# First attention of a graph network: TensorE's step in another order, key sums a step ahead of their scores, value sums five tiles behind

## The reference

```python
enh = x + 0.1 * query_emb
Q, K, V = (enh @ Wq + bq), (enh @ Wk + bk), (enh @ Wv + bv)      # 4 heads of 64
mod_k = K[src] + 0.2 * rel_w[edge_type][:, None, :]
scores = einsum('ehd,ehd->eh', Q[dst], mod_k) / 8
w = softmax of scores over the edges of one dst
agg = segment_sum(w[:, :, None] * V[src], dst)
x = layernorm(x + layernorm(agg @ Wo + bo + x) * gamma + beta)
```

## Time and profile before

| what | value |
|---|---|
| median of 3 runs | 4586.03 us (4585.14 to 4588.12) |
| profiled execution | 4583.4 us, of which span 4581.9 us |
| tiles of the first attention | 521, POOL's first gather at 350.35 us, its last at 2407.72 us |
| PE, DVE, ACT, POOL busy over the whole span | 81%, 74%, 61%, 68% |

### The profile page before, as it was taken

The page is one execution under the profiler, slowest core; times in us unless marked ns, Lnnn a source line. Parts: engine busy times, 40 slices in busy tenths (PEclk is TensorE's granted clock), DMA queues, the critical chain, the costliest instruction groups (busy, mean ns, idle before and its releaser), DMA issues. The chain is left out here.

```text
span 4581.9 us, 149697 instructions
## 1 busy us (share of the span) xinstructions
PE 3730.9 (81%) x42462; PEld 2550.6 (56%) x42462; DVE 3401.2 (74%) x11603; ACT 2779.6 (61%) x7985; POOL 3137.5 (68%) x3229
## 2 busy tenths in 40 slices
PE   6987988888888888888886877877777888778774
PEld 4654555555555555555554655555555555556553
DVE  3225788777887778877775677788877888877787
ACT  2324555555555555555553777777777777777775
POOL 1227777777777777777772777777777777777773
PEclk9998999999999999999997678777777777876876
DMA  6878998999999999898983777777777777777774
GB/s 204 281 246 238 267 267 263 264 264 264 265 263 265 263 265 266 262 265 263 265 266 100 193 206 210 204 204 206 204 207 208 204 206 206 204 207 209 204 207 129
DMA packets 820557, 1052.06 MB, mean 230 GB/s; under 512 B 458633, under 2 KB 632338, under 8 KB 820464
## 3 DMA queue, kind: packets, MB, share of 16 engines
q0 software_dynamic: 225072, 726.83, 54.0%
q1 hardware_dynamic: 594078, 323.35, 27.4%
q10 hardware_dynamic: 1314, 0.99, 0.1%
HBM read 915.79 MB, written 133.39 MB: 229 GB/s over the span
## 5 line engine op out<-in xcount | busy, mean ns | idle before, releaser
L1286 POOL DMA_INDIRECT plain_rows<-xp,plain_index x1563 | 1559.9, 998 | 555.3 <-issue 438.8
L765 POOL DMA_INDIRECT typed_rows<-kv,typed_index x1563 | 1505.2, 963 | 586.1 <-issue 444.4
L1391 PE MATMUL plain_p_o<-plain_rows,plain_weight_t 128*64 128x130 f32 (+1 forms) x8336 | 855.1, 348 | 43.3 <-DVE plain_weight_t L1417 42.5
L1158 ACT ACTIVATE typed_weight<-typed_weight,typed_col 128x416 f32<-128x416 f32 x521 | 334.7, 642 | 860.5 <-DVE typed_col L990 811.4
L1378 PE MATMUL plain_p_s<-all_cst,plain_rows 128*128 128x128 f32 (+1 forms) x2084 | 453.2, 316 | 360.0 <-DMA plain_rows<-xp,plain_index 358.1
L1391 PEld LDWEIGHTS plain_p_o<-plain_rows,plain_weight_t 128*64 128x64 f32 (+1 forms) x8336 | 569.5, 168 | 202.2 <-issue 128.7
L874 PE MATMUL typed_p_s<-typed_kt,typed_q 64*32 64x416 f32 x4168 | 471.6, 519 | 251.8 <-issue 223.4
L1378 PEld LDWEIGHTS plain_p_s<-all_cst,plain_rows 128*128 128x128 f32 (+1 forms) x2084 | 334.4, 173 | 513.2 <-issue 495.6
L988 DVE CUSTOM_DVE_ANT_0 typed_weight<-typed_p_s,typed_far 128x416 f32<-128x416 f32 x521 | 305.5, 586 | 339.5 <-PE typed_p_s L874 313.4
L1424 DVE CUSTOM_DVE_ANT_0 plain_alpha<-plain_alpha,plain_far 128x416 f32<-128x416 f32 x521 | 309.8, 595 | 309.6 <-ACT plain_alpha L1540 296.9
L961 DVE TENSOR_TENSOR typed_kt<-typed_p_kt,typed_rel 128x768 f32<-128x768 f32 x521 | 494.2, 949 | 4.0 <-PE typed_p_kt L851 3.8
(11 more groups left out here) (191 smaller groups left out, 6299.7 us busy)
## 6 DMA issues: line engine op xcount, KB each, us to landing
typed_match<-match SPq DMA_DIRECT2D x131, 208.0 KB
plain_match<-match SPq DMA_DIRECT2D x131, 208.0 KB
agg<-qkv_zero SPq DMA_DIRECT2D x98, 264.0 KB
typed_agg<-agg SPq DMA_DIRECT2D x98, 264.0 KB
plain_agg<-agg SPq DMA_DIRECT2D x98, 264.0 KB
kv<-qkv_kv SPq DMA_DIRECT2D x98, 258.0 KB
typed_kinds<-match SPq DMA_DIRECT2D x131, 192.0 KB
typed_rows<-kv,typed_index POOLq DMA_INDIRECT x1563
```

The lines of the kernel that those rows point to most:

```text
L765: pool.indirect_dma_start(rows[:, r, j, :], None, k.kv, bass.IndirectOffsetOnAxis(ap=index[:, g, at:at + 1], axis=0)).then_inc(rows_in[r], 16)
L1158: act.activation(weight[:, c], weight[:, c], ACT.Exp, bias=col[:, t.slot(4), LOW:LOW + 1]).then_inc(exp_done, 1)
L1286: pool.indirect_dma_start(rows[:, r, j, :], None, k.xp, bass.IndirectOffsetOnAxis(ap=index[:, g, at:at + 1], axis=0)).then_inc(rows_in[r], 16)
L1391: last = pe.matmul(p_o[at:at + HC, t.slot(2), 0:2 * V], weight_t[0:e, t.slot(2), j * P + at:j * P + at + HC], val[:, 2 * V * g:2 * V * g + ...
```

## The change

Three orders are rewritten. PE's step was: turned weights, sums, scores, relations, keys' transposes. It becomes: relations, keys' transposes, sums, scores, turned weights. The lags of turned weights and sums fall from 5 and 6 to 4 and 5. DVE, ACT and SP get new orders and lags to match.

```diff
-    R, M, KEY, SCORE, TURN_LAG, LAG = 8, 4, 1, 3, 5, 6
+    R, M, KEY, SCORE, TURN_LAG, LAG = 8, 4, 1, 3, 4, 5
...
-            interleave(sp, FIRST, TilePart(8, put_out), TilePart(0, fetch), BlockPart(0, 0, load), BlockPart(6, 10, store))
+            interleave(sp, FIRST, TilePart(7, put_out), TilePart(0, fetch), BlockPart(0, 0, load), BlockPart(6, 10, store))
...
             def step(t, copied=None):
-                for part in (TilePart(TURN_LAG, turn_weights), TilePart(LAG, lambda b: aggregate(b, copied)), TilePart(SCORE, score),
-                             TilePart(0, relate), TilePart(KEY, arrive)):
+                for part in (TilePart(0, relate), TilePart(KEY, arrive), TilePart(LAG, lambda b: aggregate(b, copied)),
+                             TilePart(SCORE, score), TilePart(TURN_LAG, turn_weights)):
                     part.at(t)
...
-            interleave(v, FIRST, TilePart(TURN_LAG + 2, copy_weights), TilePart(SCORE + 2, lower_bound), TilePart(0, prepare), TilePart(KEY + 2, add_keys),
+            interleave(v, FIRST, TilePart(TURN_LAG + 3, copy_weights), TilePart(1, prepare), TilePart(KEY + 2, add_keys), TilePart(SCORE + 2, lower_bound),
...
-            interleave(act, FIRST, BlockPart(2, 1, copy_message), TilePart(TURN_LAG + 1, copy_weights), TilePart(LAG + 1, put), TilePart(SCORE + 1, weigh), TilePart(1, copy_relations), TilePart(SCORE, set_apart),
+            interleave(act, FIRST, TilePart(TURN_LAG + 2, copy_weights), TilePart(SCORE + 2, weigh), BlockPart(2, 1, copy_message), TilePart(1, copy_relations), TilePart(SCORE + 1, set_apart), TilePart(LAG + 1, put),
```

## The result

| | median us | runs | ratio to before, 95% interval |
|---|---|---|---|
| before | 4586.34 | 4 (4585.14 to 4588.12) | |
| changed | 4827.49 | 4 (4820.72 to 5778.2) | 1.0518 (1.0500 to 1.0535) |

The change makes the kernel 5.2% slower, 241 us where 137 were forecast. The run of 5778.2 us had a mean granted clock of 0.598 against 0.87 in the others; the ratio leaves it out, and nothing here settles what put it there. The profiled execution took 4820.72 us.

A forecast was written before the change was run, and what follows sets the result against it. No engine is full; a ring of waits through DVE and PE bounds the first attention. 33.4 + 34.5 + 0.5 = 68.4 us for 16 tiles against 63.64; 4583.4 + 136 + 4 - 3 = 4720, quoted 4723 us, range 4655 to 4775.

The forecast's parts named there:

- the fourth rival: First attention's granted clock falls to the second attention's mix, half its time at the lower level: 5020 us; 4%.
- Turned weights last, sums five behind.: Odd tiles: sums wait for DVE's copy behind maximum and block part; normalize 4.27, join 4.45, guess 3.9, empty 3.3 us.
- 3.24 + B: Odd-tile step in us: ring of maximum, block part of length B, DVE's copy, sums, scores, next maximum.
- Keys a step ahead.: Keys' sum before DVE's maximum, scores a PE step later: 0.10 us and a wait leave; plain vary falls to 2.98.
- PE's pace and the lost lead.: Three update steps at PE's pace, 5.39 us each; two were 5.0 through PE's 0.5 us lead from the join step.
- Even tiles' copies at nothing, SP at nothing.: ACT's copies for even tiles, covered by 0.99 us of PE work, and SP's earlier `put_out` were costed at nothing.
- Loop edges.: Three waits in 16 steps right behind ends of PE's loops answer late: 0.5 us added per 16 tiles.
- The clock.: First attention: clock stays at 1.00 in the likeliest case; only a fall to the second attention's mix was priced, at 4%.
- The third rival.: Every wait of PE like one at a loop edge, copies reaching it 0.3 us late: 4770 to 4830 us; 8%.
- A wholly free POOL.: First attention's gathers without waits for PE's sums: some 72 us shorter, the most a faster ring could give.
- The signs.: Expected profile: POOL's wait for sums about 250 us; sums' wait for DVE's copy 0.7 empty, about 1.5 join and normalize.
- Early tiles and drain.: Block parts phasing in before about tile 64 cost 4 us; PE draining one step fewer at the end saves 3.

The follow-up runs named there:

- e3_fill: Changed kernel plus twelve needless matmuls of 240 columns ahead of the keys' transposes in every fourth TensorE step; 4761.03 us, ratio 1.0373.
- e8_copy_first: Changed kernel with VectorE's copy of turned weights moved right behind the maximum, ahead of the block part; 4544.3 us, ratio 0.9908.
- e2_blocks_first: Changed kernel with VectorE's block parts moved ahead of the maximum instead of behind it; 4613.4 us, ratio 1.0049.
- e4_act_copies: Changed kernel with all copies of turned weights on ScalarE, none on VectorE; 4495.95 us, ratio 0.9802.
- e6_before_act_copies: Kernel before the change with all copies of turned weights on ScalarE, nothing else changed; 4562.93 us, ratio 0.9941.

## Why the prediction was right or wrong

The direction and the mechanism were right, the size was not: 4827 us lies outside 4655 to 4775. The step that failed is the term for the clock: the sum of 68.4 us put it at nothing ("the clock stays at 1.00"), and the fourth rival had it only as a fall of the whole stage. The runs showed 3.0 us in 16 tiles, 86 us. Without that term the forecast holds: e3_fill's 4761 us less its own 0.75 us in 28.6 turns, 21 us, is 4740, inside the range.

- *Turned weights last, sums five behind.* Right. 3.24 + B gave 4.27, 4.45, 3.9 and 3.3 us; without the clock (e3_fill) normalize, join and guess measured 4.25, 4.65 and 4.02, the empty step 3.20 in the changed kernel. Join is 0.2 us longer than forecast, most of it because the join ends 2.12 us after the maximum starts (1156.20 to 1158.32), not 1.99. e8_copy_first and e2_blocks_first show that it is B in the ring that costs.
- *Keys a step ahead.* Right in kind: plain vary fell to 3.06 us where the clock held, and scores waited for no keys. With the block part out of the ring the change as a whole is worth 42 us (e8_copy_first), and with all copies on ScalarE in both kernels about 65 us (e4_act_copies against e6_before_act_copies). What the keys' place alone is worth in it no run isolates.
- *PE's pace and the lost lead.* Right: 5.34 (e3_fill) and 5.40 for 5.39.
- *Even tiles' copies at nothing, SP at nothing.* Held; all copies on ACT came in time.
- *Loop edges.* The 0.5 us can't be told apart from the join's 0.6 us in the sum: 68.4 forecast, 68.6 measured without the clock.
- *The clock.* This was taken as all or nothing: 4% for the second attention's mix over the whole stage, and nothing otherwise. It fell in between. The forecast itself named the cause, idle stretches of up to 1.5 us beside 1.1 before, and still priced the likeliest case at clock 1.00. The mean clock was 0.95. A lower clock lengthens the very links of the ring, sums and scores (1.03 and 1.54 us from start to start instead of 0.61 and 0.84 in the step shown), so join steps with a fall are 0.72 us longer than those without.
- *The third rival.* It gave 4770 to 4830 us, and 4827 lies in it, but by chance: its mechanism, an answer 0.3 us late to every copy, did not come. The sums start 0.06 us after DVE's copy ends, in join, normalize and guess steps alike.
- *A wholly free POOL.* The forecast called 72 us the most that a faster ring could give, and e4_act_copies gained 90. POOL's idle time before was 553 us from the first gather on; 1562 gaps of 0.30 us are 469 of it, so 84 us could go. The 137 waits for sums hold 68 us of it (the forecast took 72); the forecast left out that gaps put down to issue were up to 1.1 us long, 17 us in all over their 0.30. In e4_act_copies 476 us of idle time are left.
- *The signs.* POOL's wait for L888 grew from 109 to 355 us, not to 250. The sums' wait for L969 was 0.4 us in an empty step (forecast 0.7), 1.2 in normalize and 1.8 in join (forecast 1.5).
- *Early tiles and drain.* Forecast +4 and -3 us. The drain took 8 us more, and what is left of the span 3 us more.

Ring and clock, 143 + 86 us, would make the gathers 229 us longer, and they took 226; with 8 and 3 us that makes the 237 us by which the two profiled spans differ.

The fourth rival's rule was the right one to look at. The Trainium skill (TensorE: Matmul & The Clock Gate, Part 1) says that the gated clock is the default and activity releases it. e3_fill agrees: activity of no use brought the clock from 0.95 to 1.00. The stall at taken branches that the Trainium skill (Runtime: NRT & Kernel Launch, Instruction fetch mechanics) states is shown by no run.

## What to carry to other kernels

When one engine's step is reordered, write down each ring of waits with every instruction that stands in it, those queued ahead on the same engine too. A copy out of PSUM that the next matmuls need must not stand behind work that can wait: moved ahead of it, this one gave 283 us. Where a change adds idle time to TensorE in a ring that goes through its matmuls, give a partial fall of the clock its own price and chance, since it lengthens the same ring. And a lag is shared by several rings: here one fewer served the row buffers and hurt the copy, and either alone decided nothing.

## What the runs showed of the hardware

Needless bf16 matmuls, about 1.2 us of them in four of 16 steps, kept TensorE at 2.4 GHz from 700 to 2300 us and saved 66 us net. In the changed kernel PE stood idle for 1.7 to 1.9 us (once 2.2) ahead of the sums in each join step. The clock fell in or just before 44 of 67 of these steps and not about the other 23, with the same idle time, and PE was busy 83% over the stage. e8_copy_first, whose longest idle stretch of PE in that stage was 0.48 us, had no fall. e4_act_copies, busy 94%, had nine idle stretches of over 1.5 us and two falls. The indirect gathers of 128 rows on POOL, with nothing to wait for, took 0.96 us each with 0.30 us between them (e4_act_copies).
